# Reading x back block by block during the message stage of a graph attention kernel

## The reference

```python
# att: [E, 8], one weight per edge and head; h_e = x_normalised @ W_e, [8, N, 64]
msg = att[:, :, None] * jnp.transpose(h_e[:, dst], (1, 0, 2))
out = jax.ops.segment_sum(msg, src, num_segments=N)      # -> [N, 512]
x = x + out                                              # the sum that needs the node rows of x
x = x + ffn(layernorm(x))                                # gate, top 2 of 8 experts
```

## Time and profile before

| | us |
|---|---|
| median of 3 runs | 1482.93 (1481.92 to 1483.35) |
| the profiled execution, its own time | 1478.75 |
| its span, first to last instruction | 1477.0 |
| message stage, first to last matmul of line 1260 | 770.8 to 1146.0 |
| TensorE busy, share of the span | 86% |
| DVE / ACT / POOL busy | 81% / 69% / 52% |
| mean granted TensorE clock | 0.936 |

### The profile page before, as it was taken

The page is one execution under the profiler, slowest core; times in us unless marked ns, Lnnn a source line. Parts: engine busy times, 40 slices in busy tenths (PEclk is TensorE's granted clock), DMA queues, the critical chain, the costliest instruction groups (busy, mean ns, idle before and its releaser), DMA issues. The chain is left out here.

```text
span 1477.0 us, 25834 instructions
## 1 busy us (share of the span) xinstructions
PE 1275.6 (86%) x6689; PEld 747.0 (51%) x6764; DVE 1199.3 (81%) x2408; ACT 1025.5 (69%) x2477; POOL 774.9 (52%) x869
## 2 busy tenths in 40 slices
PE   6999958989999999999849799999999245999960
PEld 2455524545555555555425455555555134777740
DVE  8998788999999999999879799999999954211217
ACT  5555426878989989898849599999996243555520
POOL 2200017766666666666457577777772702665530
PEclk9999978999999999999959999999999676999985
DMA  9233339988888888888458877878773165344449
GB/s 240 94 115 124 120 129 311 320 258 285 304 288 290 291 283 295 290 296 287 126 182 254 293 245 244 246 244 245 240 247 96 43 244 198 128 135 135 128 157 345
DMA packets 141474, 324.81 MB, mean 220 GB/s; under 512 B 29794, under 2 KB 45910, under 8 KB 141226
## 3 DMA queue, kind: packets, MB, share of 16 engines
q0 software_dynamic: 62816, 212.87, 44.9%
q1 hardware_dynamic: 74138, 103.13, 20.5%
q10 hardware_dynamic: 4400, 7.34, 1.4%
HBM read 257.35 MB, written 65.93 MB: 219 GB/s over the span
## 5 line engine op out<-in xcount | busy, mean ns | idle before, releaser
L1260 PE MATMUL m_ps<-msg,hot 128*128 128x512 f32 x672 | 367.5, 640 | 11.5 <-ACT msg L1141 11.5
L1117 POOL DMA_INDIRECT rows<-he_d,target x234 | 244.8, 1046 | 105.5 <-DVE msg L1200 52.9
L998 ACT ACTIVATE rows<-rows,raw_a 128x512 f32<-128x512 f32 x336 | 273.6, 814 | 11.2
L923 PE MATMUL gs_ps<-room,hot_t 128*128 x944 | 261.9, 383 | 10.9 <-DVE hot_t L783 4.1
L996 ACT ACTIVATE rows<-d_ps 128x512 f32<-128x512 f32 x336 | 196.1, 584 | 72.9 <-PE d_ps L936 71.4
L1207 DVE TENSOR_TENSOR room<-m_ps,room 128x512 f32 x336 | 229.8, 684 | 6.2 <-PE m_ps L1260 5.1
L794 DVE TENSOR_TENSOR rows<-rows 128x512 f32<-128x512 f32 x336 | 229.4, 683 | 3.2 <-ACT rows L998 2.8
L1262 PEld LDWEIGHTS den_ps<-room,hot 128*128 128x128 f32 x672 | 128.7, 192 | 162.8 <-issue 162.8
L1200 DVE TENSOR_TENSOR msg<-rows,room 128x384 f32<-128x384 f32 x336 | 183.0, 546 | 10.8 <-DMA rows<-early_d 10.7
L762 POOL DMA_INDIRECT x_sb<-table_d,target x150 | 147.7, 985 | 80.9 <-PE d_ps L936 48.9
L1141 ACT ACTIVATE msg<-rows,room 128x64 f32<-128x64 f32 x672 | 168.2, 332 | 16.4 <-DMA rows<-early_d 16.4
(11 more groups left out here) (309 smaller groups left out, 2050.8 us busy)
## 6 DMA issues: line engine op xcount, KB each, us to landing
rows<-early_d SPq DMA_DIRECT2D x84, 256.0 KB, 3.4
early_d<-x_sb SPq DMA_DIRECT2D x51, 256.0 KB, 5.5
x_sb<-local_d SPq DMA_DIRECT2D x84, 128.0 KB, 5.3
early_d<-rows SPq DMA_DIRECT2D x33, 256.0 KB, 5.6
pair_rows<-pairs_d SPq DMA_DIRECT2D x8, 1024.0 KB, 12.9
table_d<-rows POOLq DMA_DIRECT2D x10, 520.0 KB, 3.2
both_d<-rows POOLq DMA_DIRECT2D x10, 520.0 KB, 4.2
he_d<-he SPq DMA_DIRECT2D x20, 256.0 KB, 2.0
```

What stands on the lines that cost most here:

```text
L923: pe.matmul(gs_ps[:, use(n, t) % 3, :], h, hrs[:, bass.ds(blk, 1), piece, :].rearrange("p a f -> p (a f)"), start=(piece == 0), stop=(piec ...
L998: act.activation(uv[:, j, c, :], ab[:, j, c, :], ACT.Identity, bias=raw[:, 0, c:c + 1], scale=raw[:, 1, c:c + 1]).then_inc(ur, 1)
L1117: pool.indirect_dma_start(g[:, r, t, :, :, :].rearrange("p c h d -> p (c h d)"), None, he_d, bass.IndirectOffsetOnAxis(ap=k["target"][:, q ...
L1260: pe.matmul(m_ps[:, i % BK, :], hot[:, r, t, :], msg[:, r, t, :, :, :].rearrange("p c h d -> p (c h d)"), start=True, stop=True).then_inc( ...
```

## The change

The node rows of x are read back in 20 transfers, one block each. Block b = n - 12 is issued right behind the row load of group n, from group 12 to group 31; the last block (68 rows) behind the wait on `clear`. The gate weights follow behind the row load of group 32. DVE waits for 20 x 16 counts of `xback` in place of 32.

```diff
@@ -1086,10 +1086,13 @@
                     sp.wait_ge(made, GT * (n - ROWS + 1))
                     sp.wait_ge(made_act, GT * (n - ROWS + 1))
                     sp.dma_start(g[:, r, GT - 1, :, :, :].rearrange("p c h d -> p (c h d)"), early_d[lo:lo + P, :]).then_inc(loaded[r], 16)
-                    if n == 2 * AHEAD:
-                        sp.dma_start(x_sb[:, 0:NB - 1, :], x[0:(NB - 1) * P, :].rearrange("(b p) f -> p b f", p=P)).then_inc(xback, 16)
-                        sp.wait_ge(clear, 1)
-                        sp.dma_start(x_sb[0:TAIL, NB - 1, :], x[(NB - 1) * P:N, :]).then_inc(xback, 16)
+                    b = n - 2 * AHEAD
+                    if 0 <= b < NB:
+                        if b == NB - 1:
+                            sp.wait_ge(clear, 1)
+                        rows = P if b < NB - 1 else TAIL
+                        sp.dma_start(x_sb[0:rows, b, :], x[b * P:b * P + rows, :]).then_inc(xback, 16)
+                    if b == NB:
                         sp.wait_ge(gate_made, 1)
                         sp.dma_start(wg_sb[:, :, 0:EXPERTS], wg.rearrange("(c p) e -> p c e", p=P)).then_inc(wgin, 16)
                 for b in range(0, NB, 2):
@@ -1210,7 +1213,7 @@
                 flat = rden[:, :, :].rearrange("p b h -> p (b h)")
                 link(dve.tensor_scalar(flat, den_ps[:, :], 1e-16, None, ALU.add))
                 dve.reciprocal(flat, flat).then_inc(rden_ready, 1)
-                dve.wait_ge(xback, 32)
+                dve.wait_ge(xback, 16 * NB)
```

## The result

| | before | changed |
|---|---|---|
| median, us | 1482.43 (4 runs) | 1469.45 (1465.49 to 1470.48, 4 runs) |
| profiled execution, its own time | 1478.75 | 1469.55 |
| its span | 1477.0 | 1467.8 |
| line 1260 / 1263, first to last matmul | 770.8 to 1146.0 | 771.0 to 1136.8 |
| mean granted TensorE clock | 0.936 | 0.938 |

The ratio is 0.9913, 95% interval 0.9897 to 0.993: 13 us faster, between 10.4 and 15.3. The forecast was 9.7 us faster (ratio 0.9935), 1473.2 us, so the direction is right, and the measured gain is larger; the forecast ratio lies just outside the interval.

A forecast was written before the change was run, and what follows sets the result against it. TensorE was taken to bound the message stage, interrupted once by a late row load. -8.08 - 1.62 + 0 = -9.70 us, carried from 1482.93 to 1473.2 us; range 1469.0 to 1478.0.

The forecast's parts named there:

- load 13: Message stage, row load of group 13 on SyncE behind the x read: due at 804.1, landed 29.5 us late at 836.98.
- 8.08 us of idle and 1.62 us of clock: TensorE near 830 to 842 us: one tile 8.08 us late, then two tiles 1.62 us slower at clock 0.50; together 9.70.
- the 4.2 us: Whole kernel: before's median 1482.93 over its profiled execution 1478.75, unexplained and carried over; if stall, the total would be 1469.0.
- 20 issues of 0.32 us: SyncE, groups 12 to 31: each added 256 KB read holds the queue 0.32 us, costing TensorE nothing.
- Share 0.96 to 1.00 with x in it: DMA engines, 800 to 886 us: share rises from 0.80 to 0.96 to 1.00, at 303 GB/s, against 1.03 at saturation.
- either bound (0.68 and 0.87): DMA engines' price of one more 256 KB: 0.68 us at the saturated rate, 0.87 us as today's average transfer.
- Landing 4 to 8 us: Message stage, sign in the changed trace: row loads land 4 to 8 us after issue, against 3.2 to 3.5 undisturbed.
- Rival 1: Groups 12 to 31: mix under 303 GB/s, backlog grows, second wait near 885, part of gain lost; about 1478 us, chance 0.08.
- rival 2: Groups 12 to 31: small transfers clog the DMA engines at 210 GB/s; 9 us slower, about 1492 us, chance 0.03.
- Rival 3: Load 13: stall only under the profiler, or held SyncE not the cause and pieces delay it too; 1483 us, chance 0.05.
- TensorE stays the bound: Message stage without the stall: TensorE 1.082 us a tile against DVE 1.066; 4.33 us a group against ACT 3.87.
- five groups, 21 us: Message stage: loads go out five groups of 4.33 us ahead of use, so about 21 us of lateness are free.

The follow-up runs named there:

- second and third set: Follow-up runs on other chips than the first measurements' speed: before took 1548.6 us (31 runs) in the second, 1569.7 us (19 and 23 runs) in the third.
- first set of experiments: Four follow-up runs on one chip against before (1480.1 us): x not read 1469.24, large transfer on ScalarE's queue 1468.43, at stage end 1470.24, changed kernel again 1468.42.
- third set: Runs on two chips against before (1569.7 us): each block read three times 0.9997, before again 0.9997, changed kernel 1.0000, pieces at once 0.9999.
- one pair of traces: Third set's traces of unchanged before and of the changed kernel, on two chips: message stage 425.2 and 427.3 us, ratios 0.9997 and 1.0000.

## Why the prediction was right, and where it was not

- *The large transfer held SyncE and stood in front of load 13.* Right, and shown: another queue, the end of the stage, and no x at all each remove the stall; small pieces in the same place do not (tried in the second and third set only, and seen there by the wait, since the totals tell nothing).
- *It costs TensorE 8.08 us of idle and 1.62 us of clock, and nothing wins it back.* Right where it was measured: the stage is 9.4 us shorter (375.2 to 365.8) in the first pair of traces, and its last tile starts at 1136.30 where 1135.8 was written. In the changed kernel nothing after 1136.8 gives it back: the span is 9.2 us shorter. The two parts were not tried apart.
- *The median.* The forecast 1473.2 was 3.7 us above the measured 1469.45. The profiled execution was forecast at 1469.05 and took 1469.55. The term that was mis-sized is the 4.2 us between before's profiled execution and its median, which I carried over whole: in the changed kernel the median lies 0.1 us under the profiled execution. In the first set of experiments before's median was 1480.1, 1.4 over its profiled execution, so a good part of the 4.2 us was a difference between measurements. Whether the rest is a longer stall in before's other executions, which the prediction named, no trace shows.
- *20 issues of 0.32 us.* Their median is 0.43, the longest 1.43; hidden all the same. The gate weights, priced at 3.52 us of the queue, took 0.42.
- *Share 0.96 to 1.00 with x in it.* It was 0.89 to 0.92. Against the 0.80 of the earlier trace rows, the mean of 0.90 says that one more 256 KB a group costs 0.10 x 4.33 = 0.43 us, less than either bound (0.68 and 0.87). The fit of the Trainium skill ("DMA: Bandwidth & Descriptors", section Anatomy of one DMA — SWDGE (gpsimd) path), made on transfers that GpSimd issued, gives as an estimate 2.6 us for each; the share shows no such cost as occupancy in this stage, and the same page's rule to send 1 MiB or more at a time (section Bandwidth) would have advised against a change that gains.
- *Landing 4 to 8 us.* The 20 row loads beside the reads land in 3.8 us by the median, the longest in 6.1.
- *Rival 1 and rival 2 (bandwidth, clogging).* Not seen: share stays under 1 and no second wait appears near 885. The run without x sets the bound: 365.8 us, the same.
- *Rival 3, no change.* I gave it 0.05, for reasons that were not the ones found. It is what the third set shows, and the mechanism was missing from my list: other stops, which in the one pair of traces leave TensorE idle as long without the stall as with it (8.8 us for 8.9). The step that does not carry over to those chips is "TensorE stays the bound", and with it the claim that lateness turns into time one for one. That the first measurement came from a chip at 1480 us was luck as far as the prediction goes: nothing in it told of the slower ones.

## What to carry to other kernels

A load that a pipeline needs soon should not be queued behind a long one: what counts here is how many bytes stand ahead of it in its own queue. The size of the pieces does not matter, and busy DMA engines cost it 4 to 5 us where the queue cost 29.5. Another queue or a place behind the last urgent load serves as well as cutting it up. Compute how much lateness the buffers absorb (here five groups, 21 us) before pricing the stall. And a stall is worth its length only where nothing else would have stopped the engine in that time: the 12 and 13 us of two measurements at 1480 us were 0 where other stops filled the stage. Measure on more than one chip before you count on such a gain.

## What was not expected of the hardware

- The first DMA instruction of a large read holds the queue 0.43 or 0.44 us, whatever its size (19, 15 or 10 blocks); the hold falls on the DMA instructions behind it and grows with the bytes in front. On the next row load it is 9.7 us behind 19 blocks, 2.88 behind 15 and none behind 10; on a small tail read it was 16.27; 19 pieces are held 13.4 us in sum. The line with the long hold in a profile need not be the one that caused it. GpSimd's gather issues stayed at 0.94 to 1.30 us in the same time.
- The same program took 1480, 1549 and 1570 us in three sets of runs. In the last two DVE stops for 1 to 3 us about every 15 us of the message stage (915.1, 930.3, 944.7, 960.3, 976.1 us in before of the third set), mostly "PE m_ps", though TensorE was often at work on later tiles by then, and TensorE and GpSimd then wait for DVE's messages. Two of these waits have "issue" and two "remote" as their end, so a releaser named PE need not be the cause. Each set had a chip of its own (the third had two, both at 1570), and no chip was seen at two speeds. So no run here tells what the stops are, nor whether the chip, its other cores or something else makes the difference.
